# Softmax denominators of one attention head at a time, and narrower waits, in an eight-core hybrid block

## Chip, cores and metric

The kernel runs on one Trainium2 chip, on all 8 of its cores. Each core takes one of the 8 batch elements of 2048 tokens and computes its whole output, without exchange between the cores. The metric is device time in microseconds of the slowest core.

## The reference

```python
x = L0_attn_a_x                                    # (8, 2048, 1024)
x = x + attn_a(layernorm(x), Wk, Wv, Wo, gate, freqs)   # cumulative-sum "phasor" attention
x = x + layernorm(x) @ sign(weight).T
x = x + attn_b(layernorm(x), Wq, bq, Wk, bk, Wv, bv, Wo, bo)
x = x + layernorm(x) @ sign(weight).T

def attn_b(x, ...):                                # 16 heads of 64, causal
    Q, K, V = x @ Wq.T + bq, x @ Wk.T + bk, x @ Wv.T + bv   # split into heads
    wei = where(causal, Q @ K^T / 8, -inf)
    return (softmax(wei) @ V) @ Wo.T + bo
```

The change is in attn_b, the softmax attention, alone.

## The kernel before

Everything is kept transposed in SBUF: channels on the partitions, the 2048 tokens along the rows. The program is a sequence of eight stages (layer norm, attention a, layer norm, FFN, layer norm, attention b, layer norm, FFN). A small builder keeps one list of operations for each engine. `b.op` appends to it, and each engine runs its list strictly in that order. TensorE counts its finished groups on one semaphore (T). VectorE, ScalarE and GpSimd each count every instruction on one of their own, and each waits for its own last count before its next instruction. A wait for one token of VectorE is therefore a wait for everything that was appended to VectorE's list before it, and a wait for a count that the same engine has already waited for costs no instruction: `emit` leaves it out.

Attention b (`emit_attnb`) goes over 8 pairs of heads (p). For a pair, `make_qkv_units` gives 25 units: one memset of the V tile to ones (L758), four Q units (matmuls L767, eviction L777), four K units (L790, L801) and sixteen V units (L813 and L819, eviction L828). The units of pair p+1 run between the steps of pair p, one for every two key tiles. The loops of pair p have 20 such places, so five V units remain and are run back to back at the end of the pair. The list `qkv_toks[pi]` holds their tokens in that order: memset at 0, Q at 1 to 4, K at 5 to 8, V at 9 to 24. The weights of pair p+2 are loaded by three DMAs from GpSimd's queue (`plan_w`, L213), which wait for TensorE's last group of pair p.

Within a pair, the loop qs goes over four blocks of 512 queries, and each block over its 4, 8, 12 or 16 key tiles kt. For two key tiles at a time the order is: scores of both heads (L891, L896, with the causal mask L903, L905 on the diagonal) into PC and PD; then, in the first round of a block, the normalisation of the block before; then one unit; then the products with V (`mm_av`, L868 and L872) of the tiles of the round before; then the exponentials on ScalarE (L936, L940). The V tile has a column of ones, so row 64 of POB collects the softmax denominators, head 0 in the bank PO0 and head 1 in the bank PO1.

The normalisation of a block (`make_norm`) is 32 times in the kernel (8 pairs, 4 blocks). On ScalarE it takes the logarithm of both heads' denominators (L955, 1 x 1024) and the exponential of its negative (L958, 1 x 1024). Then for each head: VectorE copies the 64 unnormalised rows out of POB (L965), TensorE spreads the reciprocals over 64 partitions with a matmul against ones (L969), and VectorE multiplies (L978). At the end a copy of the denominators' row onto itself (L988) serves as the token `norm_done`, for which the first product with V of the next block waits. All of a normalisation waits for the last product with V of its block (`av_last`). In ScalarE's list it stands ahead of the next block's first two exponentials, and in TensorE's list behind the next block's first two scores and ahead of its unit.

Of the kernel before, what the change touches and what calls it, by code (L numbers as in the profile page):

```python
# [8 lines left out]
BF16 = mybir.dt.bfloat16  # L9
I32 = mybir.dt.int32  # L10
AF = mybir.ActivationFunctionType
# [64 lines left out]
def build_program(stop_after=None):  # L76
# [34 lines left out]
    with contextlib.ExitStack() as stack:  # L111
# [8 lines left out]
        PF = e(nc.sbuf_tensor("PF32", [128, 3072], F32))  # L120
# [11 lines left out]
        ONESRB = e(nc.sbuf_tensor("ONESRB", [33, 128], BF16))  # L132
# [22 lines left out]
        UF = PF[:, 1024:2048]  # L155
        FS = PF[:, 2048:3072]
        FSB = (FS, INT[:].bitcast(F32))
        RECW = PF[0:1, 2048:3072]
        RECBW = PF[0:32, 2048:3072].bitcast(BF16)[0:1, 0:1024]
        OSCR2 = (PF[0:64, 1024:1536], PF[0:64, 1536:2048])  # L160

        PC = e(nc.psum_tensor("PC", [128, 1024], F32))
        PD = e(nc.psum_tensor("PD", [128, 1024], F32))
        POB = e(nc.psum_tensor("POB", [128, 1024], F32))
# [10 lines left out]
        b = Builder()  # L175

        for _cb in range(4):
# [3 lines left out]
                sem="dx", inc=16)  # L181
        tok_xa = b.tok("dx")
        for _cb in range(4, NB):
# [3 lines left out]
                sem="dx2", inc=16)  # L187
        tok_x = b.tok("dx2")
        tok_x_list = [tok_xa] * 4 + [tok_x] * 4
        for dst, src in ((VECS, vecs_d), (TROW, trow_d), (ISQ, isq_d),  # L190
# [4 lines left out]
             sem="dw", inc=16, is_dma=True)  # L195
        tok_consts = b.tok("dc")
# [12 lines left out]
            sem=None, inc=0)  # L209
# [513 lines left out]
        def emit_attnb(ln_toks):  # L723
# [122 lines left out]
            for p in range(NB):  # L846
                pi = p % 2
                QTp, KTp, VSB = QT2[pi], KT2[pi], VSB2[pi]
                qt_all = list(qkv_toks[pi]) + [tok_consts]
                prev_qs_exp = pair_end_T[1 - pi]  # L850
                prev_qs_av = pair_end_T[1 - pi]
                for qs in range(4):
                    av_toks = {}
                    exp_toks = []
# [3 lines left out]
                    def plan_av(kt, qs=qs, nkt=nkt, VSB=VSB,  # L858
                                av_toks=av_toks):
                        diag = kt >= 4 * qs  # L860
                        qoff = 128 * kt if diag else 512 * qs
                        N = (512 * (qs + 1) - 128 * kt) if diag else 512
                        ep = (EPA, EPB, EPC, EPD)[kt % 4]

                        def mm_av(t, kt=kt, qs=qs, ep=ep, qoff=qoff, N=N,
                                  nkt=nkt, VSB=VSB):
                            o = qoff - 512 * qs
                            t.matmul(PO0[0:65, o:o + N],  # L868
                                     VSB[:, kt * 130:kt * 130 + 65],
                                     ep[:, 0:N],  # L870
                                     start=(kt == 0), stop=(kt == nkt - 1))
                            return t.matmul(  # L872
                                PO1[0:65, o:o + N],
                                VSB[:, kt * 130 + 65:kt * 130 + 130],
                                ep[:, 512:512 + N],
                                start=(kt == 0), stop=(kt == nkt - 1))
                        wav = [exp_toks[kt]]
                        if kt == 0 and norm_done is not None:
                            wav.append(norm_done)
                        av_toks[kt] = b.op("tensor", mm_av, wait=wav,  # L880
                                           sem="T", inc=1)

                    for kc in range(0, nkt, 2):
                      for kt in (kc, kc + 1):
                        diag = kt >= 4 * qs
                        qoff = 128 * kt if diag else 512 * qs
                        N = (512 * (qs + 1) - 128 * kt) if diag else 512
                        ps = PC if kt % 2 == 0 else PD
                        def mm_s(t, ps=ps, kt=kt, qoff=qoff, N=N, diag=diag,
                                 QTp=QTp, KTp=KTp):  # L890
                            t.matmul(ps[:, 0:N],  # L891
                                     KTp[0:64, kt * 128:kt * 128 + 128],
                                     QTp[0:64, qoff:qoff + N],
                                     start=True, stop=not diag,
                                     tile_position=(0, 0))
                            ins = t.matmul(  # L896
                                ps[:, 512:512 + N],
                                KTp[64:128, kt * 128:kt * 128 + 128],
                                QTp[64:128, qoff:qoff + N],
                                start=True, stop=not diag,  # L900
                                tile_position=(64, 0))
                            if diag:
                                t.matmul(ps[:, 0:128], IDENTB[:], MASKB[:],  # L903
                                         start=False, stop=True)
                                ins = t.matmul(ps[:, 512:640], IDENTB[:],  # L905
                                               MASKB[:], start=False,
                                               stop=True)
                            return ins
                        w = list(qt_all)
                        if kt >= 2:  # L910
                            w.append(exp_toks[kt - 2])
                        elif prev_qs_exp is not None:
                            w.append(prev_qs_exp)
                        ts_ = b.op("tensor", mm_s, wait=w, sem="T", inc=1)
                        exp_toks.append([ts_, None])
# [7 lines left out]
                      for kt in (kc, kc + 1):  # L923
# [14 lines left out]
                        else:  # L938
                            def do_exp(s, ps=ps, ep=ep, N=N):
# [6 lines left out]
                                  inc=0)  # L946
# [5 lines left out]
                    prev_qs_av = av_toks[nkt - 1]  # L952
                    def make_norm(p=p, qs=qs, av_last=av_toks[nkt - 1]):
                        def run():
                            r0 = b.op("scalar", lambda s: s.activation(  # L955
                                RECW, POB[64:65, 0:1024], AF.Ln),
                                wait=[av_last], sem=None, inc=0)
                            r1 = b.op("scalar", lambda s: s.activation(  # L958
                                RECBW, RECW, AF.Exp, scale=-1.0),
                                wait=[r0], sem=None, inc=0)  # L960
                            nts = []
                            for hh, po in ((0, PO0), (1, PO1)):
                                OSCR = OSCR2[hh]
                                c1 = b.op("vector", lambda v, po=po,
                                          OSCR=OSCR: v.tensor_copy(  # L965
                                              OSCR, po[0:64, 0:512]),
                                          wait=[av_last], sem=None, inc=0)
                                tr1 = b.op("tensor", lambda t, po=po,
                                           hh=hh: t.matmul(  # L969
                                               po[0:64, 0:512],  # L970
                                               ONESRB[0:1, 0:64],
                                               RECBW[:, hh * 512:
                                                     hh * 512 + 512],
                                               start=True, stop=True),
                                           wait=[r1, c1], sem="T", inc=1)
                                nt = b.op("vector", lambda v, p=p, qs=qs,
# [8 lines left out]
                                nts.append(nt)  # L985
                                big_toks.append(nt)
                            fin = b.op("vector", lambda v, nts=nts:
                                       v.tensor_copy(RECW, RECW),  # L988
                                       wait=nts, sem=None, inc=0)
                            return fin  # L990
                        return run
# [113 lines left out]
```

How the kernel before makes its waits and increments, by code:

```python
            def run(eng):  # L49
                hi = {}
                chain_pos = {}
                for fn, waits, sem, inc, chain in self.events[eng_name]:
                    if chain:
                        k = chain_pos.get(chain, 0)
                        if k > 0:
                            eng.wait_ge(sems[chain], k)
                        chain_pos[chain] = k + 1
                    for ws, wv in waits:
                        if wv > 0 and hi.get(ws, 0) < wv:
                            eng.wait_ge(sems[ws], wv)
                            hi[ws] = wv
                    ins = fn(eng)
                    if inc:
                        ins.then_inc(sems[sem], inc)
                    elif chain:
                        ins.then_inc(sems[chain], 1)
                return None
```

## Time and profile before

| what | value |
|---|---|
| median of 2 runs, slowest core | 1726.97 us (1726.84 to 1727.11) |
| profiled execution, its own time | 1739.62 us |
| span of the profiled core (core 6) | 1738.0 us |
| spans of the eight cores | 1713.1 to 1738.0 us |
| TensorE (PE) busy | 1030.9 us, 59% |
| VectorE (DVE) busy | 844.2 us, 49% |
| ScalarE (ACT) busy | 629.3 us, 36% |
| GpSimd (POOL) busy | 57.0 us, 3% |
| mean granted TensorE clock, core 6 | 0.770 |
| attention b, first to last normalisation | 858.9 to 1533 us |

A granted clock of 1.00 is TensorE's 2.4 GHz, one of 0.50 is 1.2 GHz. The rows of the trace are those of core 6, the slowest in the profiled execution, unless a group says otherwise. The number in brackets at the end of a row is how long the engine stood idle before that instruction, and what released it.

### The profile page before, as it was taken

How to read it: one execution, taken by the hardware profiler on the slowest of the kernel's cores; microseconds unless marked ns; L12 is line 12 of the kernel's file. 1: busy time of each engine (PE TensorE's matmuls, PEld its weight loads, DVE VectorE, ACT ScalarE, POOL GpSimd, SP SyncE). 2: the span in 40 equal slices, each digit the busy share in tenths (PEclk: the TensorE clock that was granted, in tenths of full speed). 3: DMA queues.
4: the chain of work that ended last, by engine and by line, in shares of the span. 5: the costliest groups of instructions: out<-in, count | busy, mean ns of one | idle time of the engine just before them, and what ended most of it. 6: DMA issues, size and time to landing. Idle time of an engine off the chain costs nothing.

```text
span 1738.0 us, 16120 instructions; the slowest of 8 cores (1713.1 to 1738.0 us)
## 1 busy us (share of the span) xinstructions
PE 1030.9 (59%) x5088; PEld 431.1 (25%) x5088; DVE 844.2 (49%) x1072; ACT 629.3 (36%) x683; POOL 57.0 (3%) x69
## 2 busy tenths in 40 slices
PE   0444443432312942942887878787878787777458
PEld 0111111111101410410433333333333333233123
DVE  1367889888897346347423223222322223135453
ACT  0535433343320051051154545554545456712300
POOL 1000000000000100001000000000000000010000
PEclk9767676675655975975887878787878788788679
DMA  9003213311010400104002020202020200032025
GB/s 243 0 1 32 23 18 37 36 12 12 0 13 0 37 1 12 37 1 37 1 1 19 1 18 1 19 1 19 1 19 1 19 1 1 1 29 20 1 72 171
DMA packets 73155, 42.03 MB, mean 24 GB/s; under 512 B 67696, under 2 KB 67696, under 8 KB 71024
## 3 DMA queue, kind: packets, MB, share of 16 engines
q0 software_dynamic: 66592, 16.78, 11.0%
q1 hardware_dynamic: 6480, 24.21, 4.6%
q8 instruction: 43, 0.70, 0.2%
q14 instruction: 40, 0.33, 0.1%
HBM read 47.28 MB, written 10.49 MB: 33 GB/s over the span
## 4 chain that ended last, share of the span: by engine, by line
PE 45%; DVE 29%; ACT 12%; DMA 6%; issue 5%; DVEq 1%; SPq 1%; POOL 1%; ACTq 0%; POOLq 0%
PE PC L625 7%; PE PC L693 5%; PE PRB L767 5%; PE PRB L790 4%; PE POB L868 4%; PE PRB L813 4%; PE POB L872 3%; DVE LNT L380 3%; DVE POOLBF L375 3%; ACT POOLBF L261 3%; PE PD L499 2%; PE PC L891 2%; DVE POOLBF L544 2%; DVE POOLBF L563 2%; DVE POOLBF L569 2%
## 5 line engine op out<-in xcount | busy, mean ns | idle before, releaser
L936 ACT ACTIVATE POOLBF<-PC 128x1024 bf16<-128x1024 f32 x128 | 131.0, 1023 | 210.7 <-PE PC L896 124.0
L261 ACT ACTIVATE POOLBF<-LNT 128x2048 bf16<-128x2048 bf16 x32 | 61.1, 1910 | 236.2 <-DVE LNT L255 232.1
L868 PE MATMUL POB<-POOLBF 128*65 128x512 bf16 (+1 forms) x320 | 122.4, 387 | 3.7 <-DVE PF L988 3.7
L828 DVE CAST POOLBF<-PRB 128x128 bf16<-128x128 f32 x128 | 37.7, 295 | 178.3 <-PE PRB L819 176.9
L872 PE MATMUL POB<-POOLBF 128*65 128x512 bf16 (+1 forms) x320 | 116.5, 379 | 0.0
L936 ACT ACTIVATE POOLBF<-PD 128x1024 bf16<-128x1024 f32 x96 | 98.2, 1023 | 15.0 <-ACT POOLBF L936 0.9
L499 PE MATMUL PD<-LNT,WSB 128*128 128x512 bf16 x128 | 39.2, 475 | 92.7 <-ACT POOLBF L507 92.7
L969 PE MATMUL POB<-PF,ONESRB 1*64 1x512 bf16 x64 | 30.8, 482 | 106.0 <-DVE PF L965 55.0
L282 PE MATMUL POB<-LNT,ONESB 128*1 128x512 bf16 x128 | 41.0, 478 | 85.2 <-DVE LNT L255 85.2
L978 DVE TENSOR_TENSOR BIG<-PF,POB 64x512 bf16<-64x512 f32 x64 | 43.5, 680 | 90.1 <-PE POB L969 90.1
L625 PE MATMUL PC<-BIG,WSA 128*128 128x512 bf16 x256 | 60.0, 395 | 45.6 <-DVE BIG L581 39.9
L693 PE MATMUL PC<-LNT,WSA 128*128 128x512 bf16 x256 | 64.4, 414 | 24.7 <-DVE XT L703 15.2
L703 DVE TENSOR_TENSOR XT<-XT,PC 128x512 f32<-128x512 f32 x64 | 44.0, 688 | 70.8 <-PE PC L693 70.1
L499 PE MATMUL PD<-LNT,WSA 128*128 128x512 bf16 x128 | 36.4, 449 | 68.2 <-ACT POOLBF L507 68.2
L342 PE MATMUL PRB<-PF,ONESRB 1*128 1x512 bf16 x16 | 8.5, 531 | 111.4 <-ACT PF L334 111.4
L459 PE MATMUL PC<-LNT,WSA 128*128 128x512 bf16 x128 | 44.5, 524 | 46.7 <-DMA WSA<-wv 26.8
L965 DVE COPY PF<-POB 64x512 f32<-64x512 f32 x64 | 43.7, 682 | 57.9 <-PE POB L872 53.9
L891 PE MATMUL PC<-POOLBF 64*128 64x512 bf16 (+1 forms) x160 | 66.7, 417 | 6.0 <-DVE POOLBF L828 5.2
L777 DVE TENSOR_SCALAR POOLBF<-PRB,DER 128x512 bf16<-128x512 f32 x32 | 24.0, 751 | 91.8 <-PE PRB L767 88.2
L459 PE MATMUL PC<-LNT,WSB 128*128 128x512 bf16 x128 | 42.1, 504 | 43.7 <-DMA WSB<-wv 26.6
L955 ACT ACTIVATE PF<-POB 1x1024 f32<-1x1024 f32 x32 | 32.5, 1016 | 97.4 <-PE POB L872 97.4
L896 PE MATMUL PC<-POOLBF 64*128 64x512 bf16 (+1 forms) x160 | 67.0, 418 | 0.0
(146 smaller groups left out, 2125.3 us busy)
## 6 DMA issues: line engine op xcount, KB each, us to landing
XT<-xT SPq DMA_DIRECT2D x8, 1024.0 KB, 17.3
yT<-XT SPq DMA_DIRECT2D x8, 1024.0 KB, 5.5
BIG<-wts POOLq DMA_DIRECT2D x8, 256.0 KB, 7.2
wsgn<-BIG SPq DMA_DIRECT2D x8, 256.0 KB, 2.6
WSA<-wsgn SPq DMA_DIRECT2D x8, 256.0 KB, 4.3
WSB<-wsgn SPq DMA_DIRECT2D x8, 256.0 KB, 4.5
WSA<-wk POOLq DMA_DIRECT2D x4, 256.0 KB, 5.5
WSA<-wv POOLq DMA_DIRECT2D x4, 256.0 KB, 7.5
```

Of the source, the lines that this page charges most:

```text
L261: tk = b.op("scalar", lambda s, cb=cb: s.activation(SQF[:, cb * T:(cb + 1) * T], LNT[:, cb * T:(cb + 1) * T], AF.Square), wait=[copy_toks[ ...
L459: ins = t.matmul(PC[:, (s4 % 2) * 512:(s4 % 2) * 512 + 512], ws[:, i * 128:i * 128 + 128], LNT[:, i * T + s4 * 512: i * T + s4 * 512 + 512 ...
L499: ins = t.matmul(PD[:, (s4 % 2) * 512:(s4 % 2) * 512 + 512], ws[:, 1024 + i * 128:1024 + i * 128 + 128], LNT[:, i * T + s4 * 512:i * T + s ...
L625: ins = t.matmul(PC[:, (s4 % 2) * 512:(s4 % 2) * 512 + 512], ws[:, i * 128:i * 128 + 128], BIG[:, i * T + s4 * 512:i * T + s4 * 512 + 512] ...
L693: ins = t.matmul(PC[:, (s4 % 2) * 512:(s4 % 2) * 512 + 512], ws[:, i * 128:i * 128 + 128], LNT[:, i * T + s4 * 512:i * T + s4 * 512 + 512] ...
L767: ins = t.matmul(prr[:], ws[:, i * 128:i * 128 + 128], LNT[:, i * T + s4 * 512: i * T + s4 * 512 + 512], start=(i == 0), stop=(i == NB - 1))
L790: ins = t.matmul(prr[:], ws[:, 1024 + i * 128:1024 + i * 128 + 128], LNT[:, i * T + s4 * 512: i * T + s4 * 512 + 512], start=(i == 0), sto ...
L813: t.matmul(prr[:, 0:128], LNT[:, i * T + tt * 128: i * T + tt * 128 + 128], ws[:, 2048 + i * 128:2048 + i * 128 + 128], start=(i == 0), st ...
L868: t.matmul(PO0[0:65, o:o + N], VSB[:, kt * 130:kt * 130 + 65], ep[:, 0:N], start=(kt == 0), stop=(kt == nkt - 1))
L872: return t.matmul(PO1[0:65, o:o + N], VSB[:, kt * 130 + 65:kt * 130 + 130], ep[:, 512:512 + N], start=(kt == 0), stop=(kt == nkt - 1))
L891: t.matmul(ps[:, 0:N], KTp[0:64, kt * 128:kt * 128 + 128], QTp[0:64, qoff:qoff + N], start=True, stop=not diag, tile_position=(0, 0))
L936: return s.activation(ep[:, 0:1024], ps[:, 0:1024], AF.Exp)
```

## The change

It changes three things in attention b.

1. The normalisation takes the logarithm and the exponential for one head at a time: Ln (1 x 512) and Exp (1 x 512) of head 0, then the same of head 1, each just ahead of its head's operations. There are four ScalarE instructions for each block in place of two. The matmul that spreads head 0's reciprocals waits for head 0's Exp alone. The scratch rows move: `RECW` and `RECBW` become `REC2` and `RECB2`, one pair for each head, and `OSCR2` moves to other columns of the same buffer. The closing copy is 1 x 512 in place of 1 x 1024.
2. The scores wait for the Q tile of their block, the K tile of their four key tiles and the constants, in place of all 25 units of the pair.
3. The product with V of key tile kt waits for V tile kt as well.

```diff
-        RECW = PF[0:1, 2048:3072]
-        RECBW = PF[0:32, 2048:3072].bitcast(BF16)[0:1, 0:1024]
-        OSCR2 = (PF[0:64, 1024:1536], PF[0:64, 1536:2048])
+        REC2 = (PF[0:1, 2048:2560], PF[0:1, 0:512])
+        RECB2 = (PF[0:32, 2048:2560].bitcast(BF16)[0:1, 0:512],
+                 PF[0:32, 0:512].bitcast(BF16)[0:1, 0:512])
+        OSCR2 = (PF[0:64, 2560:3072], PF[0:64, 1024:1536])
@@
-                        wav = [exp_toks[kt]]
+                        wav = [exp_toks[kt], qt_all[9 + kt]]
@@
-                        w = list(qt_all)
+                        w = [qt_all[1 + qs], qt_all[5 + kt // 4],
+                             tok_consts]
@@
                         def run():
-                            r0 = b.op("scalar", lambda s: s.activation(
-                                RECW, POB[64:65, 0:1024], AF.Ln),
-                                wait=[av_last], sem=None, inc=0)
-                            r1 = b.op("scalar", lambda s: s.activation(
-                                RECBW, RECW, AF.Exp, scale=-1.0),
-                                wait=[r0], sem=None, inc=0)
                             nts = []
                             for hh, po in ((0, PO0), (1, PO1)):
+                                REC = REC2[hh]
+                                RECB = RECB2[hh]
                                 OSCR = OSCR2[hh]
+                                r0 = b.op("scalar", lambda s, po=po, REC=REC:
+                                          s.activation(
+                                              REC, po[64:65, 0:512],
+                                              AF.Ln), wait=[av_last],
+                                          sem=None, inc=0)
+                                r1 = b.op("scalar", lambda s, REC=REC,
+                                          RECB=RECB: s.activation(
+                                              RECB, REC, AF.Exp,
+                                              scale=-1.0),
+                                          wait=[r0], sem=None, inc=0)
                                 c1 = b.op("vector", lambda v, po=po,
                                           OSCR=OSCR: v.tensor_copy(
                                               OSCR, po[0:64, 0:512]),
                                           wait=[av_last], sem=None, inc=0)
                                 tr1 = b.op("tensor", lambda t, po=po,
-                                           hh=hh: t.matmul(
+                                           RECB=RECB: t.matmul(
                                                po[0:64, 0:512],
-                                               ONESRB[0:1, 0:64],
-                                               RECBW[:, hh * 512:
-                                                     hh * 512 + 512],
+                                               ONESRB[0:1, 0:64], RECB,
                                                start=True, stop=True),
                                            wait=[r1, c1], sem="T", inc=1)
@@
                             fin = b.op("vector", lambda v, nts=nts:
-                                       v.tensor_copy(RECW, RECW),
+                                       v.tensor_copy(REC2[0], REC2[0]),
                                        wait=nts, sem=None, inc=0)
```

## Rows read from the trace of the kernel before

**Rows 1.** The page's chain that ended last, share of the span by engine.

```profile
...
PE 45%; DVE 29%; ACT 12%; DMA 6%; issue 5%; DVEq 1%; SPq 1%; POOL 1%; ACTq 0%; POOLq 0%
...
```

**Rows 2.** The view of the cores: span in us, mean granted clock.

```profile
...
core 0: 1716.1 us, clock 0.777
...
core 6: 1738.0 us, clock 0.770
...
```

**Rows 3.** The waits, 855 to 1533 us: us in total, times, longest us.

```profile
...
PE POB L969 <- DVE PF L965: 55.0, 32, 1.7
...
PE POB L969 <- ACT PF L958: 51.0, 25, 2.6
...
PE PRB L767 <- DMA WSB<-wvbT: 15.0, 3, 5.6
PE PRB L767 <- DMA WSA<-wvbT: 14.9, 3, 5.3
...
PE POB L868 <- DVE PF L988: 3.7, 4, 1.0
...
```

**Rows 4.** Timeline of one normalisation: start us, us, engine, line, instruction [idle before].

```profile
...
1079.04 1.02 ACT L955 ACTIVATE PF<-POB 1x1024 f32<-1x1024 f32 x1 [1.06 <-PE POB L872]
...
1080.20 1.05 ACT L958 ACTIVATE PF<-PF 1x1024 bf16<-1x1024 f32 x1
1081.41 1.02 ACT L936 ACTIVATE POOLBF<-PC 128x1024 bf16<-128x1024 f32 x1
...
1081.52 0.37 PE L969 MATMUL POB<-PF,ONESRB 1*64 1x512 bf16 x1 [2.03 <-ACT PF L958]
1081.99 0.68 DVE L978 TENSOR_TENSOR BIG<-PF,POB 64x512 bf16<-64x512 f32 x1 [2.26 <-PE POB L969]
...
1082.78 0.68 DVE L965 COPY PF<-POB 64x512 f32<-64x512 f32 x1
...
1083.61 0.60 PE L969 MATMUL POB<-PF,ONESRB 1*64 1x512 bf16 x1 [1.72 <-DVE PF L965]
...
1085.32 0.60 PE L891 MATMUL PC<-POOLBF 64*128 64x512 bf16 x1
...
```

**Rows 5.** Groups of instructions by line and form, ScalarE and VectorE: busy us, mean ns.

```profile
...
L334 ACT ACTIVATE PF<-PF 1x512 bf16<-1x512 f32 x16 | 10.0, 628 | 2.3
...
L311 ACT ACTIVATE PF<-POB 1x512 f32<-1x512 f32 x16 | 9.4, 587 | 1.7
...
L988 DVE COPY PF<-PF 1x1024 f32<-1x1024 f32 x32 | 22.0, 687 | 8.1 <-DVE BIG L978 8.1
...
```

**Rows 6.** Timeline, last V unit of a pair and what follows it.

```profile
...
1019.50 0.29 DVE L828 CAST POOLBF<-PRB 128x128 bf16<-128x128 f32 x1 [0.41 <-PE PRB L819]
1019.89 0.68 DVE L965 COPY PF<-POB 64x512 f32<-64x512 f32 x1
1019.94 0.88 POOL L213 DMA_DIRECT2D WSB<-wqT  x1 [86.30 <-PE PRB L819]
...
1020.04 0.37 PE L891 MATMUL PC<-POOLBF 64*128 64x512 bf16 x1 [0.65 <-DVE POOLBF L828]
...
```

**Rows 7.** Windows on core 6: length, busy us of PE, PEld, DVE, ACT, POOL, granted clock.

```profile
...
1038.00:1046.00 8.00, 6.28 (x18) 1.74 (x18) 3.47 (x5) 2.94 (x4) 0.00 (x0) 0.57 0.00 0
...
1083.00:1091.00 8.00, 7.39 (x41) 3.35 (x42) 2.42 (x6) 3.62 (x4) 0.00 (x0) 0.57 0.00 0
...
```

**Rows 8.** The same view on core 0.

```profile
...
1036.00:1042.00 6.00, 6.00 (x22) 1.94 (x22) 2.11 (x3) 1.92 (x2) 0.00 (x0) 0.72 0.00 0
...
```

**Rows 9.** Timeline of ScalarE on core 6, two Ln that follow each other.

```profile
...
1035.43 1.02 ACT L955 ACTIVATE PF<-POB 1x1024 f32<-1x1024 f32 x1 [9.76 <-PE POB L872]
...
1055.33 1.02 ACT L955 ACTIVATE PF<-POB 1x1024 f32<-1x1024 f32 x1 [2.07 <-PE POB L872]
...
```

**Rows 10.** The same view on core 0.

```profile
...
1031.33 1.02 ACT L955 ACTIVATE PF<-POB 1x1024 f32<-1x1024 f32 x1 [7.56 <-PE POB L872]
...
1050.30 1.02 ACT L955 ACTIVATE PF<-POB 1x1024 f32<-1x1024 f32 x1 [2.07 <-PE POB L872]
...
```

## The prediction

> **What bounds the kernel now.** I began with the page's chain that ended last: TensorE holds 45% of it, VectorE 29%, ScalarE 12% [rows 1]. TensorE is the main link, but over half of the chain is work for which TensorE stands still. The change touches attention b alone, so I read the view of the waits for that stretch. TensorE's waits at L969, the matmul that spreads the reciprocals, are its largest there: 51.0 us in 25 places until ScalarE's Exp, and 55.0 us in 32 places until VectorE's copy [rows 3]. There are 32 normalisations. In 25 of them the first L969 waits for ScalarE, in the other 7 it does not. Next comes the wait of the first Q unit for its weights, 29.9 us in 6 places, 5.0 us each [rows 3].
>
> The timeline of one normalisation shows the order. All times here count from the start of the Ln. The Ln runs to 1.02, the Exp from 1.16 to 2.21, the first L969 starts at 2.48, VectorE's multiply at 2.95, its copy for head 1 at 3.74, and the second L969 at 4.57. Then come the unit and the next scores, at 6.28 [rows 4]. It is one chain, with TensorE idle for 2.03 and 1.72 us in it. All that follows in TensorE's list stands behind the second L969.
>
> **Ln and Exp of head 0 alone.** This is the part that pays. The new forms are 1 x 512. The nearest rows are a ScalarE copy out of PSUM of 1 x 512 at 0.587 us, and an Exp of just the new form at 0.628 us [rows 5]. From Ln to Exp there are 0.14 us between the end of one and the start of the next [rows 4]. The first Exp ends at 0.59 + 0.14 + 0.63 = 1.36 in place of 2.21, so the first L969 comes 0.85 us earlier. VectorE's copy of head 0 takes 0.68 from about 0 and does not come in between.
>
> Everything behind is a chain at fixed durations, so the second L969 moves from 4.57 to 3.72, if head 1's Exp is there. It is: its Ln starts at 1.36 + 0.14 = 1.50, and its Exp ends at 1.50 + 1.36 = 2.86. With the 0.27 us that lie between Exp and L969 in the row, 3.13 would do. Head 1's part costs nothing as long as VectorE's multiply and copy (1.4 us) cover it. Without that cover it would cost nearly the whole 0.85.
>
> A bound from below for the Ln: if the part that does not scale were larger than in the copy, it could cost the whole 1.02 less a little, and the gain would be 0.43. From above: the Ln of 1 x 1024 takes 1.02, the copy of half as many 0.59, and this difference per element fits the Exp pair too (1.05 and 0.63), so no more than 0.9 is to be had. I take 0.85.
>
> It counts 25 times: 21.3 us. The 7 others are those at the start of pairs 1 to 7. There the Ln starts while TensorE still works through five V units, and VectorE's copy stands in its list behind the last V eviction: eviction at 1019.50, copy at 1019.89, scores at 1020.04 [rows 6]. ScalarE has long finished, and a shorter Ln moves nothing. In 6 of these 7 the first Q unit then waits for its weights, whose DMA started with the end of TensorE's V units (GpSimd's row at 1019.94). That is untouched too.
>
> **ScalarE's two added instructions.** The next block's first exponential starts at 2.37 now [rows 4], and after four instructions at 2 x (0.59 + 0.14 + 0.63 + 0.14) = 3.00, so 0.63 later. It ends at 4.03. Who waits for it are the scores of key tile 2, which need PC. They start at 6.28 now and at 5.43 after, so 1.4 us of cover are left. The second exponential ends at about 5.2, and its scores come 0.4 us behind the first ones, at 5.8. In pair 7 there are no units, and these scores could start right behind the second L969, at 4.2: the first has no cover to speak of, the second is held back by about 1 us. But there the products with V that follow are released by the closing copy, so I charge nothing for that.
>
> **The closing copy.** It is on the path 4 times (3.7 us of waits at L868 [rows 3]), all in pair 7 as I read it, since there no unit stands between. It takes 0.69 us at 1 x 1024 [rows 5]; at 512 it saves between nothing and 0.34. I take 0.25, times 4: 1.0 us.
>
> **The scores' narrower wait.** Within a pair nothing changes, for the wait had been met before the pair's first scores. At the start of a pair the scores no longer wait for the last V eviction. TensorE is idle for 0.65 us there [rows 6], of which up to 0.5 can go. In six pairs the weights' 5.0 us hide it. In pairs 0 and 7 it counts: 0.8 us together, between nothing and 1.3.
>
> **The products' added wait.** From pair 1 on the wait for `norm_done`, appended to VectorE's list later, includes it; in pair 0 all V evictions stand in the lists before the first scores. It holds nothing up: nothing.
>
> **TensorE's clock.** Behind a normalisation the granted clock is 0.50. It means 0.57 over the 8.0 us from 1083, which is 2 x 0.43 x 8.0 = 6.9 us at the 1.2 GHz level, and the same at 1038 [rows 7]. The two idle stretches of 2.03 and 1.72 us [rows 4] came before it fell. On core 0 one such stretch is shorter: 0.72 over 6.0 us, so 3.4 us at the lower level [rows 8]. What this is worth shows in the distance from that block's Ln to the next: 19.90 us on core 6, where it is long [rows 9], and 18.97 us on core 0, where it is short [rows 10]. So a short stretch in place of a long one gives back 0.93 us.
>
> With the change the idle time in a normalisation goes from 3.75 to 2.90 us, and TensorE is dense again 0.85 us sooner. That is not nothing, so the clock still falls, I think. But it can rise one step sooner behind some. If none does: 0. If all 25 do: 23 us. I take one in four, 6 us, an estimate.
>
> The Trainium skill (TensorE: Matmul & The Clock Gate, Why this matters for your kernels) says that the clock falls where there are long idle gaps between bursts of matmuls, and gives a length longer than either gap here. The trace disagrees: the clock falls in a normalisation whose longest gap is 2.03 us. By the page read as it stands there would be no low stretch now, and nothing to win from shorter gaps: the sum would be 23.1 us and the time 1704, inside the forecast's own bounds.
>
> **The sum.** 21.3 + 1.0 + 0.8 = 23.1 us, and 6 from the clock: 29. The profiled execution took 1739.6 us (span 1738.0) and would take 1711. The median of the runs shown is 12.6 us lower. I put this down to the weights' waits on the slowest cores, for core 0 spans 1716.1 and core 6 1738.0 [rows 2], which the change leaves alone. So the same 29 come off the median: 1727 - 29 = 1698.
>
> **Rivals.**
> *The clock comes back too.* The low stretch becomes short behind most normalisations: 23.1 + 20 = 43, so 1684. For it: TensorE is busy in 7.39 of 8.0 us behind the normalisation at 1083 [rows 7], so little was missing for an earlier rise. Against it: core 0 has the short stretch with the same instructions [rows 8], so it hangs on when the gap comes, and a gap that comes sooner can be hit either way. Chance 0.15.
> *The gain is absorbed.* The blocks end sooner, but the clock's low stretches get longer behind those where they were short, and the pairs still start by their weights. Then half of the 23 us stays, 1715. For it: core 0 has a stretch of 3.4 us where core 6 has 6.9 [rows 7, 8], so a shift in time can double one. Against it: the weights' DMA starts with the pair's end and moves along. Chance 0.12.
> *ScalarE becomes the path.* If the scores behind a normalisation waited for the first exponential, each would come 0.63 us later in place of 0.85 earlier: 26 x 0.63 = 16, so 1743. This decides once the exponential's end at 4.03 slips past the scores' start at 5.43, that is, if the four short instructions took 1.4 us more than their rows say. A switch of function tables between Ln and Exp would do that, but between them lie 0.14 us now, with no load in the row [rows 4]. Chance 0.04.
>
> **How the numbers follow.** The forecast, the chain's 23 us and anything from 0 to 12 from the clock, is 1692 to 1704 and has 0.69; its own bounds (Ln at 0.43 in place of 0.85) reach to 1711. Range: 1686 to 1711, which leaves out most of the absorbed case, the slower one, and half of the large return of the clock. About what a measurement of this kernel can tell from no change is 2%, here 34.5 us. Faster by over 2% means under 1692.4: the return of the clock and a part of the forecast's edge, 0.20. Slower by over 2% needs 1761.5: 0.02. Within: 0.78.
>
> **What would show it.** Right: the waits at L969 on the Exp fall from 2.04 us to about 1.2 each and stay 25; those on VectorE's copy stay at 1.72; from a block's first Ln to its second L969 it is 3.7 us; the new Ln and Exp take 0.59 and 0.63; the first exponential starts at 3.0. The time between starts of pairs falls by 2.6 us, or by 3.5 with the clock's part. Wrong: a wait of the second L969 for ScalarE, a wait of L891 for L936 behind a unit, or distances between blocks that shrink by much more or less than 0.85 us, where the granted clock in the windows behind the normalisations tells whether it was the clock.

## The result and the profile after

The changed kernel takes 1703.99 us (median of 11 runs), the kernel before 1726.97 us (median of 10). The ratio is 0.984 with a 95% interval of 0.980 to 0.988, that is 20 to 35 us less. Beside its variants on another chip it came to 0.984 again (0.978 to 0.990). The single medians lie 23 us apart and include runs that the chip disturbed; the ratio does not. The change is clearly faster, by about 2% or less.

The profile is that of core 7 now, the slowest, with a span of 1696.0 us. First the view of the waits over attention b: line, what it waited for, us in total, times, longest.

```profile
...
PE POB L977 <- DVE PF L973: 55.0, 32, 1.7
...
PE POB L977 <- ACT PF L968: 29.8, 25, 1.7
...
PE PRB L768 <- DMA WSA<-wvbT: 14.7, 3, 6.0
PE PRB L768 <- DMA WSB<-wvbT: 14.1, 3, 5.6
...
PE POB L869 <- DVE PF L994: 0.4, 1, 0.4
...
```

The spreading matmul (L969 before, L977 now) waits for the Exp in 25 places as before [rows 3], but for 29.8 us in place of 51.0. The wait for VectorE's copy is 55.0 us as it was. The pair starts' wait for weights is 28.8 us on this core, against 29.9 on core 6 before. The closing copy no longer holds up the products with V: 0.4 us in 1 place, against 3.7 in 4.

The timeline of one normalisation (start us, us, engine, line, instruction, idle before):

```profile
...
1058.05 0.59 ACT L963 ACTIVATE PF<-POB 1x512 f32<-1x512 f32 x1 [1.06 <-PE POB L873]
...
1058.78 0.63 ACT L968 ACTIVATE PF<-PF 1x512 bf16<-1x512 f32 x1
1059.51 0.59 ACT L963 ACTIVATE PF<-POB 1x512 f32<-1x512 f32 x1
...
1059.67 0.37 PE L977 MATMUL POB<-PF,ONESRB 1*64 1x512 bf16 x1 [1.18 <-ACT PF L968]
...
1060.24 0.63 ACT L968 ACTIVATE PF<-PF 1x512 bf16<-1x512 f32 x1
1060.93 0.68 DVE L973 COPY PF<-POB 64x512 f32<-64x512 f32 x1
1061.02 1.02 ACT L938 ACTIVATE POOLBF<-PC 128x1024 bf16<-128x1024 f32 x1
...
1061.76 0.60 PE L977 MATMUL POB<-PF,ONESRB 1*64 1x512 bf16 x1 [1.72 <-DVE PF L973]
...
1063.38 0.41 DVE L994 COPY PF<-PF 1x512 f32<-1x512 f32 x1 [0.24 <-DVE BIG L984]
...
1063.47 0.60 PE L892 MATMUL PC<-POOLBF 64*128 64x512 bf16 x1
...
```

Counted from the first Ln at 1058.05, the first spreading matmul starts at 1.62 us and the second at 3.71, against 2.48 and 4.57 in [rows 4]. Head 1's Exp (1060.24 to 1060.87) ends 0.89 us before the second matmul starts. The first exponential of the next block starts at 2.97 in place of 2.37, and the scores of key tile 2 at 5.42 in place of 6.28. ScalarE ends that exponential at 1062.04, 1.4 us before these scores. The closing copy takes 0.41 us.

The clock, in the view of windows (length, busy us of PE, PEld, DVE, ACT, POOL, granted clock), first behind the normalisation just shown, then behind another:

```profile
...
1061.00:1069.00 8.00, 7.24 (x41) 3.35 (x42) 2.33 (x6) 5.06 (x5) 0.00 (x0) 0.58 0.00 0
939.00:946.00 7.00, 6.59 (x35) 2.67 (x36) 2.86 (x5) 4.29 (x5) 0.00 (x0) 1.00 0.00 0
...
```

Behind the Ln at 1058.05 the clock falls as before: 0.58 over 8 us is 2 x 0.42 x 8 = 6.7 us at the 1.2 GHz level. Behind the Ln at 935.70 it never falls. How far apart the blocks are shows what that is worth:

```profile
...
935.70 0.59 ACT L963 ACTIVATE PF<-POB 1x512 f32<-1x512 f32 x1 [7.89 <-PE POB L873]
...
952.19 0.59 ACT L963 ACTIVATE PF<-POB 1x512 f32<-1x512 f32 x1 [2.06 <-PE POB L873]
...
1036.39 0.59 ACT L963 ACTIVATE PF<-POB 1x512 f32<-1x512 f32 x1 [2.06 <-PE POB L873]
...
1058.05 0.59 ACT L963 ACTIVATE PF<-POB 1x512 f32<-1x512 f32 x1 [1.06 <-PE POB L873]
...
```

From 935.70 to 952.19 there are 16.49 us, for the block in the same place of a pair that took 19.90 on core 6 before [rows 9]. A block without any fall is the exception: of the seven in this place (pairs 0 to 6) it is one on core 7, three on core 0 and none on core 2. From 1036.39 to 1058.05 there are 21.66, for the block that took 1079.04 - 1055.33 = 23.71 before [rows 4, 9].

The slowest core alone gives too large a picture of the gain. From the first Ln to the last, attention b took 667.7 us on cores 6 and 7 before and 647.1 to 647.9 on the other six. Cores 6 and 7 waited 29.9 and 32.3 us for weights at the starts of pairs, the others 14.7 to 21.2. With the change it takes 616.6 to 633.2 us on the eight cores, and they wait 23.6 to 32.8 us for weights. So cores 6 and 7 gain 39 and 34.5 us, and cores 0 to 5 gain 16 to 31, 22.5 in the mean. Each of these is one execution.

### The profile page after: what moved, and what is told of

It is laid out like the page before. It is cut to its first block, busy times and chain, and to the rows that moved or that the text cites. A ratio compares the mean times of both kernels' runs of the same rounds, so it can differ in the third digit from the quotient of the medians.

```text
span 1696.0 us, 16297 instructions; the slowest of 8 cores (1680.3 to 1696.0 us)
## 1 busy us (share of the span) xinstructions
PE 1020.8 (60%) x5088; PEld 430.4 (25%) x5088; DVE 835.7 (49%) x1072; ACT 642.2 (38%) x747; POOL 56.9 (3%) x69
## 4 chain that ended last, share of the span: by engine, by line
PE 47%; DVE 29%; ACT 12%; issue 5%; DMA 5%; DVEq 1%; POOL 1%; SPq 1%; ACTq 0%; POOLq 0%
PE PC L626 7%; PE PC L694 6%; PE PRB L768 5%; PE POB L869 4%; PE PRB L791 4%; PE PRB L814 4%; PE POB L873 4%; DVE POOLBF L376 3%; DVE LNT L381 3%; ACT POOLBF L262 3%; PE PD L500 2%; PE PC L892 2%; DVE POOLBF L570 2%; DVE POOLBF L564 2%; DVE POOLBF L545 2%
## 5 line engine op out<-in xcount | busy, mean ns | idle before, releaser
L938 ACT ACTIVATE POOLBF<-PC 128x1024 bf16<-128x1024 f32 x128 | 131.2, 1025 | 158.4 <-PE PC L897 79.4
L938 ACT ACTIVATE POOLBF<-PD 128x1024 bf16<-128x1024 f32 x96 | 98.4, 1025 | 14.4 <-PE PRB L820 0.4
L977 PE MATMUL POB<-PF,ONESRB 1*64 1x512 bf16 x64 | 28.3, 442 | 85.4 <-DVE PF L973 55.0
L963 ACT ACTIVATE PF<-POB 1x512 f32<-1x512 f32 x64 | 37.8, 590 | 95.5 <-PE POB L873 92.6
L460 PE MATMUL PC<-LNT,WSA 128*128 128x512 bf16 x128 | 44.4, 524 | 38.2 <-DMA WSA<-wv 20.4
L892 PE MATMUL PC<-POOLBF 64*128 64x512 bf16 (+1 forms) x160 | 64.7, 404 | 2.0 <-ACT POOLBF L938 0.8
L897 PE MATMUL PC<-POOLBF 64*128 64x512 bf16 (+1 forms) x160 | 64.9, 405 | 0.0
```

The source lines that it names most:

```text
L460: ins = t.matmul(PC[:, (s4 % 2) * 512:(s4 % 2) * 512 + 512], ws[:, i * 128:i * 128 + 128], LNT[:, i * T + s4 * 512: i * T + s4 * 512 + 512 ...
L892: t.matmul(ps[:, 0:N], KTp[0:64, kt * 128:kt * 128 + 128], QTp[0:64, qoff:qoff + N], start=True, stop=not diag, tile_position=(0, 0))
L938: return s.activation(ep[:, 0:1024], ps[:, 0:1024], AF.Exp)
```

## The experiments

The theory: the gain is the chain's, 25 normalisations in which the second spreading matmul starts 0.85 us earlier, and a few us from the clock; the narrower waits give almost nothing. The rivals: the waits carry a part that counts; the smaller instructions pay by themselves; the clock is the real cause, or none of it. All ratios are to the kernel before, on the same chip, with 95% intervals. The variants ran on three chips, so a difference between two of their ratios is less certain than either alone. A difference in ratio is turned into us with the 1727 us of the kernel before. Where a `diff` below is written in words (for each head: ...), it tells the order of the operations and is not the code.

**The parts apart.** First the change without its waits, that is, with these two edits undone:

```diff
-                        wav = [exp_toks[kt], qt_all[9 + kt]]
+                        wav = [exp_toks[kt]]
@@
-                        w = [qt_all[1 + qs], qt_all[5 + kt // 4],
-                             tok_consts]
+                        w = list(qt_all)
```

> The change without its waits: Ln and Exp by head, the smaller closing copy, but the scores and the products with V wait as in the kernel before. Theory (the first head's shorter Ln and Exp carry the gain, the waits nearly none): the ratio to the kernel before stays within 0.3% of the full change's 0.984, so 0.981 to 0.987, and the waits of L969's successor for the Exp are 25 of 1.2 us. Rival (the narrower waits carry a part that counts): 0.99 or more.

Measured: 0.981 (0.975 to 0.986). The wait for the Exp:

```profile
...
PE POB L976 <- DVE PF L972: 55.0, 32, 1.7
...
PE POB L976 <- ACT PF L967: 29.8, 25, 1.7
...
```

It is 29.8 us in 25 places, to the tenth that of the full change. The split of the Ln and the Exp, with its smaller closing copy, carries all of the gain that can be measured. Then the waits alone, the same two edits made in the kernel before:

> The waits alone: the normalisation stays as in the kernel before. Theory: no more than 1 us, ratio 0.998 to 1.001, since six of eight pair starts are hidden under the weights' wait. Rival (the waits carry part of the gain): 0.995 or less.

Measured: 0.997 (0.994 to 1.001), which is not told apart from no change. It lies just below the theory's 0.998 to 1.001, and the rival's 0.995 lies inside the interval too, so how much the waits give, up to some 10 us by this run alone, is not settled by it. But the variant above, with the full gain and without the waits, leaves little for them. At a pair's start in the changed kernel the scores start 0.04 us behind the start of the last V eviction, as against 0.54 in [rows 6]:

```profile
...
1003.32 0.29 DVE L829 CAST POOLBF<-PRB 128x128 bf16<-128x128 f32 x1 [0.41 <-PE PRB L820]
...
1003.36 0.37 PE L892 MATMUL PC<-POOLBF 64*128 64x512 bf16 x1
...
1003.72 0.68 DVE L973 COPY PF<-POB 64x512 f32<-64x512 f32 x1
...
1003.76 0.88 POOL L214 DMA_DIRECT2D WSB<-wqT  x1 [78.23 <-PE PRB L820]
...
```

The wait is gone, as the diff says. VectorE's copy (1003.72) and GpSimd's DMA (1003.76) come where they did, 0.40 and 0.44 us behind that eviction's start.

**The same instructions in another order.** The changed kernel with ScalarE's list as Ln, Ln, Exp, Exp:

```diff
-  for each head: Ln; Exp; copy; spreading matmul; multiply
+  for each head: Ln
+  for each head: Exp
+  for each head: copy; spreading matmul; multiply
```

> The full change, but with ScalarE's four instructions in the order Ln, Ln, Exp, Exp. The first head's Exp then ends about 2.1 us after the start of the Ln, as against 2.21 in the kernel before and 1.36 in the changed one, while ScalarE carries the same four instructions. Theory (the start of the first head's spreading matmul is what counts, ScalarE's added 0.63 us is hidden): ratio 0.995 to 1.000. Rival 1 (the smaller forms or the smaller closing copy pay by themselves): near 0.984 as the full change. Rival 2 (ScalarE's added time costs something that the full change hid by its gain): above 1.002.

Measured: 0.996 (0.993 to 0.999).

```profile
...
PE POB L988 <- DVE PF L984: 53.3, 31, 1.7
...
PE POB L988 <- ACT PF L974: 46.8, 25, 2.4
...
```

The wait for the Exp is 46.8 us, 4.2 less than before, and the time is 0.4% less, some 7 us. The kernel has the small forms, the small closing copy and all four ScalarE instructions, and three quarters of the gain are gone. So it is the start of the first spreading matmul, with the chain behind it, that pays, and not the sizes. ScalarE's 0.6 us more per normalisation cost nothing that shows.

**More of the same: the second matmul.** If the second spreading matmul sets what follows, moving it further must pay at the same rate. In the changed kernel with VectorE's two copies ahead of its two multiplies it waits for head 1's Exp alone:

```diff
-  for each head: Ln; Exp; copy; spreading matmul; multiply
+  for each head: copy
+  for each head: Ln; Exp; spreading matmul; multiply
```

> The changed kernel with VectorE's two copies out of POB ahead of both multiplies. The second spreading matmul then no longer waits for copy 2 behind multiply 1; the last to come is the second head's Exp, 2.86 us after the start of the first Ln, so the matmul starts at about 3.13 in place of 3.72. Theory (the time of the second spreading matmul sets what follows, at face value): 25 x 0.59 = 15 us less than the changed kernel, ratio to the kernel before 0.971 to 0.978, and its wait is for ScalarE now. Rival (what the changed kernel won it won with the first matmul alone): no less than the changed kernel.

Measured: 0.973 (0.968 to 0.977). The timeline, with the Ln at 1059.31:

```profile
...
1059.31 0.59 ACT L973 ACTIVATE PF<-POB 1x512 f32<-1x512 f32 x1 [1.06 <-PE POB L873]
1059.32 1.47 DVE L964 COPY PF<-POB 64x512 f32<-64x512 f32 x2 [0.91 <-PE POB L873]
...
1060.93 0.37 PE L983 MATMUL POB<-PF,ONESRB 1*64 1x512 bf16 x1 [1.18 <-DVE PF L964]
...
1062.38 0.37 PE L983 MATMUL POB<-PF,ONESRB 1*64 1x512 bf16 x1 [1.08 <-ACT PF L978]
...
```

The second matmul starts at 3.07 us and waits for ScalarE. It moved by 0.64 us, 25 x 0.64 = 16 us; from 0.984 to 0.973 are 19 to 20 us. And in the kernel before, with the wide Ln and Exp and the wide waits left alone, and only the two copies first:

```diff
-  Ln and Exp of both heads; for each head: copy; spreading matmul; multiply
+  Ln and Exp of both heads; for each head: copy
+  for each head: spreading matmul; multiply
```

> The kernel before, Ln and Exp for both heads at once and all its waits, with the two copies ahead of the multiplies and nothing else. The first spreading matmul stays at 2.48 us, the second follows at once, at about 2.9 in place of 4.57. Theory (the second matmul counts): 25 x 1.67 = 42 us less at unchanged clock, ratio 0.965 to 0.977, better than the change itself, though no Ln or Exp is shorter. Rival (the first matmul's start counts): 0.998 to 1.002.

Measured: 0.963 (0.959 to 0.968). The middle is just below the range of the theory, the interval reaches into it. Its timeline, with the Ln at 1056.98:

```profile
...
1056.98 1.02 ACT L955 ACTIVATE PF<-POB 1x1024 f32<-1x1024 f32 x1 [1.06 <-PE POB L872]
1056.99 1.47 DVE L966 COPY PF<-POB 64x512 f32<-64x512 f32 x2 [0.91 <-PE POB L872]
...
1059.46 0.59 PE L973 MATMUL POB<-PF,ONESRB 1*64 1x512 bf16 x2 [2.03 <-ACT PF L958]
...
1059.97 0.62 PE L813 MATMUL PRB<-WSB,LNT 128*128 128x128 bf16 x8
...
1060.68 0.39 PE L891 MATMUL PC<-POOLBF 64*128 64x512 bf16 x1
...
1061.69 0.58 PE L891 MATMUL PD<-POOLBF 64*128 64x512 bf16 x1 [0.61 <-ACT POOLBF L936]
...
```

The two spreading matmuls now run as one group from 2.48 us on. No Ln or Exp is any shorter, and the gain is more than double that of the change: 63 us, where the theory put 42. The rows show why it is more. The unit starts at 2.99, and in the kernel before it started at 5.10 (1084.14), so the chain gives 25 x 2.11 = 53 us; the theory had counted 1.67 for each. And the unit takes 0.71 us from its start to the next scores, where it took 1.18: TensorE's granted clock is 1.00 from 1060 to 1061 here, and in the kernel before it is 0.50 from 1084 to 1086, under the same unit and scores. That is 25 x 0.47 = 12 us if it is so behind all 25. The two make 65. Behind the unit the clock falls as before: it is 0.57 over the 8 us from 1060. The first of the next scores come at 3.70 in place of 6.28. The last row shows what is late next: the second scores wait 0.61 us for ScalarE's first exponential.

**The clock by itself.** The kernel before with eight unread matmuls ahead of the first spreading matmul. It computes nothing new and brings none of its other work forward:

```diff
+  for _ in range(8):
+      t.matmul(PR[:], MASKB[:], LNT[:, 0:512], start=True, stop=True)
   for each head: copy; spreading matmul; multiply
```

> The kernel before with eight matmuls of 128x512, whose results nobody reads, ahead of the first spreading matmul of each normalisation. They run while TensorE would wait for ScalarE (2.03 us) and so leave the chain's times as they are: only TensorE's idle time goes from 3.75 to about 2 us. What changes is the clock's doing. Theory (the clock's low stretches behind normalisations cost 0.93 us for each that is shortened and more where the fall goes away): the granted clock behind normalisations rises and the time falls by 10 to 45 us, ratio 0.974 to 0.994. Rival (the clock's part is nothing, the blocks are bound by ScalarE anyway): 0.998 to 1.002. If the filler itself gets in the way of the chain: above 1.002, with a later start of the spreading matmul.

Measured: 0.978 (0.974 to 0.983). From its timeline, with the Ln at 1062.19, and the window behind:

```profile
...
1062.19 1.02 ACT L955 ACTIVATE PF<-POB 1x1024 f32<-1x1024 f32 x1 [1.06 <-PE POB L872]
...
1062.56 1.90 PE L963 MATMUL PRB<-LNT,MASKB 128*128 128x512 bf16 x8
1063.35 1.06 ACT L958 ACTIVATE PF<-PF 1x1024 bf16<-1x1024 f32 x1
...
1064.66 0.37 PE L977 MATMUL POB<-PF,ONESRB 1*64 1x512 bf16 x1 [0.20 <-ACT PF L958]
...
1066.76 0.37 PE L977 MATMUL POB<-PF,ONESRB 1*64 1x512 bf16 x1 [1.72 <-DVE PF L973]
...
1067.77 0.39 PE L891 MATMUL PC<-POOLBF 64*128 64x512 bf16 x1
...
```

```profile
...
1066.00:1074.00 8.00, 7.25 (x46) 3.10 (x46) 2.85 (x6) 4.81 (x5) 0.00 (x0) 0.79 0.01 2
...
```

The spreading matmuls start at 2.47 and 4.57 us, just where they did in the kernel before [rows 4]. Yet the scores start at 5.58 in place of 6.28, because the unit ran at full clock. In the window, which starts 3.8 us behind its Ln (the one at 1083 did by 4.0), the clock is 0.79 in place of 0.57: 3.4 us at the lower level in place of 6.9 [rows 7]. The next Ln comes at 1086.45, so this block is 24.3 us long, where the same block of pairs 0 to 6 took 25.5 to 25.9 on core 6 before. What filled the gap brings none of the other work forward, so the 37 us (29 to 45 by the interval) come by the clock. It is worth more here than the whole change is.

Two things have to be told apart from it. First, the slowest cores before were those that waited longest for weights. But the gain is there without them: on cores 0 to 5, where the waits for weights are alike (18.8 us before, 17.9 here in the mean), attention b goes from 647.4 to 619.2 us, 28 less. Second, the filler is not hidden everywhere. In 23 of the 25 normalisations the spreading matmul still waits for the Exp behind it (5.3 us in total on core 7), but in the 7 at the starts of pairs TensorE does not stand idle ahead of the first spreading matmul, and the filler stands in its way: on core 7 it runs for 1.89 us from 1009.18, and the spreading matmul starts behind it at 1011.00. So the 28 us are what is left after up to 7 x 1.9 = 13 us for that, and the clock's part is larger than the gain shows.

To see whether chain and clock are two gains or one, the changed kernel with a filler of four such matmuls:

```diff
+  for _ in range(4):
+      t.matmul(PR[:], MASKB[:], LNT[:, 0:512], start=True, stop=True)
   for each head: Ln; Exp; copy; spreading matmul; multiply
```

> The changed kernel with four unread matmuls of 128x512 ahead of the first spreading matmul, in the 1.2 us in which TensorE waits for the first Exp. The same filler idea gave the kernel before a ratio of 0.978. Theory (the chain's 0.85 us and the clock are two separate parts, and the chain's part is still there when the clock is mostly out of play): 25 x 0.85 = 21 us below the kernel before with its filler, ratio to the kernel before 0.962 to 0.970. Rival (the change and the filler win the same thing, the clock): 0.975 or more.

Measured: 0.965 (0.961 to 0.968). The rival's 0.975 is excluded: the change and the filler do not win the same thing. It is 0.0135 below the filler alone, 23 us, where 25 x 0.85 = 21 us of chain were put. The agreement is better than the comparison can bear. The two ratios are of different chips, and their intervals leave 10 us either way. The fillers differ too: four matmuls stand in the way half as long at the starts of pairs as eight, and the clock is lower with them, as the view of windows over attention b shows:

```profile
...
856.00:1470.00 614.00, 518.22 (x3143) 230.64 (x3143) 182.46 (x328) 359.31 (x440) 15.79 (x18) 0.89 0.09 9
...
```

It is 0.89 here and 0.92 with the filler of eight (shown at the end), against 0.81 before and 0.84 with the change. That the two gains add in full (0.984 and 0.978 would make 0.962) is within the interval, and not shown more closely than that.

**A version that beats both.** The wide Ln and Exp, both copies first, the narrower waits, and the unit ahead of the spreading matmuls in TensorE's list, so that real work stands in the place of the filler:

```diff
-  Ln, Exp; for each head: copy; spreading matmul; multiply; then the unit
+  Ln, Exp; for each head: copy; then the unit
+  for each head: spreading matmul; multiply
```

> A version meant to beat both: Ln and Exp for both heads at once, both copies first, and the next unit of Q, K or V ahead of the two spreading matmuls in TensorE's list, so that it fills the time in which TensorE would wait for ScalarE. The narrower waits of the change are in. Theory: the scores of key tile 2 wait for ScalarE's first exponential (end at 3.39 us after the Ln) and start near 3.5 in place of 6.28 in the kernel before, and the clock keeps its upper level behind most normalisations; 2.8 x 24 = 67 us and 10 to 30 us from the clock, ratio 0.94 to 0.965. Rival (ScalarE, with two exponentials behind the Ln and the Exp, becomes the bound as soon as TensorE's idle time is gone): 0.97 or more, no better than the variants without the unit ahead.

Measured: 0.957 (0.952 to 0.962), only 0.007 better than the copies first alone, and the intervals of the two overlap. The waits over attention b tell why:

```profile
...
PE PD L891 <- ACT POOLBF L940: 22.9, 36, 1.1
...
PE POB L978 <- ACT PF L962: 20.3, 25, 2.6
...
PE PRB L767 <- DMA WSB<-wvbT: 16.3, 3, 5.5
PE PRB L767 <- DMA WSA<-wvbT: 15.9, 3, 5.7
...
PE PC L891 <- ACT POOLBF L940: 11.6, 24, 0.8
...
```

The wait for the Exp is 20.3 us now, down from 51.0. The scores wait 34.5 us for ScalarE's exponentials, which was 5.1 for the same lines in the kernel before. ScalarE has become the next link, so the rival was right in part. The weights' 32.2 us are nearly as much. In the last kernel they are loaded a pair earlier:

```diff
-                free_ws[pi] = b.tok("T")
-                plan_w(p + 2)
+                free_ws[1 - pi] = b.tok("T")
+                plan_w(p + 3)
```

with the load for pair 2 ahead of the loop.

> The version with the unit ahead, and the weights of a pair's Q, K and V loaded one pair earlier, as soon as TensorE has read the ones that they replace. Theory (the six pair starts wait about 5 us each for weights, and nothing else stands behind that wait): these waits vanish, 6 x 3 to 5 us = 18 to 30 us less than the unit ahead alone (0.957), ratio 0.938 to 0.948. Rival (the pair starts' normalisation, until now hidden by that wait, takes its place): 0.95 or more.

Measured: 0.929 (0.925 to 0.933), a median of 1614.8 us. That is below the forecast of 0.938 to 0.948. Attention b waits for no weights of Q, K or V any more. By the ratios the step is 0.028 or 48 us, more than the 32 us of the waits, but it compares two chips, and the profiled execution of the kernel ahead of it was 10 us faster (1647.3 us) than the median of its runs (1657.7). The two profiled executions lie 34 us apart (1647.3 and 1613.4), and attention b is 36 us shorter in the mean of the cores, where the waits were 31.7. So the waits explain all but some 4 us of it, and the rest of the 48 is not shown by a trace.

## Why the prediction was right, and where it was off

Its 1698 stands against 1704, or by the ratio 1727 x 0.984 = 1700, in the range 1686 to 1711. The chain, the main term, is right in size and cause. That the total comes so close is in part luck: the clock gave more than the 6 us that it was put at, and longer waits for weights and a smaller gain in pair 7 took some of it back.

**Right, the chain.** The step from 2.48 to 1.63 for the first spreading matmul and from 4.57 to 3.72 for the second was measured as 1.62 and 3.71. The wait for the Exp fell by 21.2 us in 25 places, where 21.3 were forecast. The forms had been priced from ScalarE's 1 x 512 rows [rows 5], and they came out so:

```profile
...
L968 ACT ACTIVATE PF<-PF 1x512 bf16<-1x512 f32 x64 | 40.4, 631 | 9.9 <-ACT PF L963 0.9
...
L963 ACT ACTIVATE PF<-POB 1x512 f32<-1x512 f32 x64 | 37.8, 590 | 95.5 <-PE POB L873 92.6
...
L994 DVE COPY PF<-PF 1x512 f32<-1x512 f32 x32 | 13.5, 421 | 8.1 <-DVE BIG L984 8.1
...
```

0.590 for the Ln, where the copy had 0.587, and 0.631 for the Exp, where 0.628 had been read. The closing copy saves 0.27 us in place of 0.25. Head 1's part is covered: the second matmul's 32 waits are all for VectorE. The 7 normalisations that were counted as nothing still wait for VectorE, not for the Exp.

**Right, ScalarE's two instructions.** The cover of 1.4 us was there, and the order Ln, Ln, Exp, Exp shows that they cost nothing that can be measured. The scores' own waits for ScalarE's full exponentials (L936 before, L938 now) are 7.1 us in place of 5.1.

**Off: pair 7.** Without units the chain was to give 0.85 there and the closing copy 0.25 for each block, 3.3 us over the three blocks between its four Ln. They are 2.1 us shorter on core 7 and 3.0 on core 6. The first of them is shorter by 0.3 only. The prediction had weighed that scores are held back there and charged nothing for it; whether that is the cause is not shown.

**Off: the clock's term.** The step said that a shortened low stretch gives back 0.93 us, and took one in four, 6 us. Both numbers were too low for what is seen in attention b. From the first Ln to the last, core 6 had 1526.54 - 858.87 = 667.7 us before, and core 7 now has 1488.0 - 854.8 = 633.2. Of these 34.5 us, 24 x 0.85 = 20.4 are the chain, and about 1.4 the closing copies and the start of pair 7, an estimate. The other 12 to 13 are the clock and the landing of the weights, and the latter moved by 1.1. In the row pair above, 23.71 - 21.66 = 2.05 us, of which 1.2 are the clock's, and this block takes 21.6 to 21.7 us in 6 of 7 pairs on core 7. And the step said "the clock still falls, I think". In most normalisations it does, in the one at 935.70 it does not, and 19.90 - 16.49 = 3.41 us are the 0.85 of the chain and 2.56 of the clock. The sign that was named for it, starts of pairs 3.5 us closer together, came out as 3.2 to 7.3 us between core 6 before and core 7 now. Over attention b the granted clock of the slowest core is 0.81 before and 0.84 now:

```profile
...
859.00:1526.00 667.00, 521.77 (x3019) 227.36 (x3016) 190.50 (x328) 347.74 (x378) 15.78 (x18) 0.81 0.08 8
...
855.00:1488.00 633.00, 513.26 (x3022) 226.50 (x3018) 182.17 (x328) 359.75 (x440) 15.79 (x18) 0.84 0.09 8
...
```

The mechanism was right, and its size is the term that was mis-sized: 6 forecast, about 11 found on the slowest core, by what is left over and not by a run of its own. The filler shows what the rows of before could not: some 37 us, net of the filler's own cost, are there to be had from the clock, where the rival "the clock comes back too" put 20. The change gets to some 11 of them.

**Off: the weights.** The prediction held their waits to be untouched. On the slowest core they are. But on cores 0 to 5 they went from 18.8 us in the mean to 27.1, and this took back 8.3 of what chain and clock had given there. The sum comes out so: these cores gained 22.5 us, and with the 8.3 that is 31, of which 20.4 are the chain, 1.4 the small terms and 9 the clock.

**Open.** This accounts for most of the gap between the 34.5 to 39 us by which attention b is shorter on cores 6 and 7, and the 20 to 35 us by which the whole kernel is. The profiled execution of the kernel before was 12.6 us above its median, and it was slow on just those two cores. Whether the change itself lengthens the waits for weights is not known. With the same chain and without the narrower waits they were 23.7 us in the mean of the eight cores, in the kernel before 21.8 and in the changed one 28.0, each in a single execution.

**The rule on gaps.** The changed kernel has its two gaps at 1.18 and 1.72 us, and the clock falls behind most of them all the same. The rule that was weighed in the prediction (the Trainium skill, TensorE: Matmul & The Clock Gate, Why this matters for your kernels) would have no fall here, neither before nor after, if single long gaps were the only thing that counts. The measurement decides against reading it so: gaps that are each short can let the clock fall.

## What to carry to other kernels

Follow a small chain between engines to the link behind which everything else is queued, and price the whole list in front of it, not the instruction that looks slow. Here the second matmul waited for a copy that was only late because it stood behind a multiply. Putting two copies first gave 3.7%, where halving the Ln and the Exp gave 1.6%. Where TensorE stands idle in short gaps, put unread matmuls there as a probe: they give a price for the clock apart from the chain, and tell whether it pays to move real work into the gap. Where TensorE is not idle they stand in its way, and that cost has to be added back. And compare all cores, not the slowest alone: here two of the eight had a different wait of their own before.

## What the runs showed of the hardware that was not expected

- Unread matmuls, hidden in most of 32 places and in the way in at least 7, made a kernel 2.2% faster through the granted clock: over 859 to 1484 us on the slowest core it is 0.92, where it was 0.81 over the same stage before.

```profile
...
859.00:1484.00 625.00, 532.33 (x3269) 238.81 (x3267) 190.37 (x328) 347.77 (x379) 15.80 (x18) 0.92 0.09 9
...
```

- The clock can fall behind two gaps of 1.18 and 1.72 us with one matmul between them, and behind the very same gaps it can stay up. The same block is then 16.49 us long or 18.07 to 19.56, in steps.
- Ln out of PSUM for 1 x 512 costs the same as a copy of that form (0.590 and 0.587 us), and between Ln and Exp lie 0.14 us, between Exp and the next Ln 0.10 us, with no table load between them in the rows shown.
